# Moving the third gate and up group of a slot ahead of k and q, from tile 8 on, in a fused retention and feed-forward block

## What is computed

```python
q1, k1 = x @ Wq, x @ Wk                 # 4 heads of 64, then rotary
v = x @ Wv                              # 4 heads of 128
o = chunk_retention(q * 64 ** -0.5, k, v, gamma)
o = rmsnorm(o, gn_weight) * silu(x @ Wg)
x = layernorm(x + o @ Wo)
h = silu(x @ wg.T) * (x @ wu.T)         # 768 hidden, int weights / 127
x = layernorm(x + h @ wd.T)
```

## Time and profile before

| | |
|---|---|
| median of 3 runs | 443.9 us (443.34 to 444.12) |
| the profiled execution's own time | 444.02 us |
| its span, first to last instruction | 442.2 us |
| PE busy | 428.2 us (97%) |
| PE weight loads busy | 400.4 us (91%) |
| DVE busy | 302.1 us (68%) |
| ACT busy | 295.7 us (67%) |
| POOL busy | 238.9 us (54%) |
| mean granted TensorE clock | 0.997 |

### The profile page before, as it was taken

One profiled execution on the slowest core, in us unless ns is written; L12 is line 12 of the kernel. 1 busy time (PEld: TensorE's weight loads), 2 busy tenths in 40 slices (PEclk: granted clock), 3 DMA queues, 4 the chain that ended last, 5 costly groups with the idle time before them and its releaser, 6 DMA issues.

```text
span 442.2 us, 10997 instructions
## 1 busy us (share of the span) xinstructions
PE 428.2 (97%) x3552; PEld 400.4 (91%) x3552; DVE 302.1 (68%) x857; ACT 295.7 (67%) x891; POOL 238.9 (54%) x381
## 2 busy tenths in 40 slices
PE   7989999999999999999999999999999999999994
PEld 3878889999999999999999999999999999999983
DVE  4989566657766776666776667677666667766774
ACT  5678766657766767765776676686676667665541
POOL 2654255755555465453766446564655546554564
PEclk9999999999999999999999999999999999999998
DMA  7931000011100111110111101011110000100011
GB/s 241 363 134 50 0 29 22 24 38 37 38 11 27 37 38 38 37 37 0 36 36 36 36 27 44 0 36 36 36 36 13 15 22 14 38 12 13 14 38 39
DMA packets 16228, 19.60 MB, mean 44 GB/s; under 512 B 1472, under 2 KB 13760, under 8 KB 16192
## 3 DMA queue, kind: packets, MB, share of 16 engines
q1 hardware_dynamic: 16192, 19.14, 13.2%
HBM read 14.94 MB, written 4.19 MB: 43 GB/s over the span
## 4 chain that ended last, share of the span: by engine, by line
PE 85%; DVE 8%; issue 3%; POOL 1%; ACT 1%; DMA 1%; SPq 0%; POOLq 0%; DVEq 0%; ACTq 0%
PE b_rows L440 28%; PE b_ffn L440 18%; PE b_rows L458 8%; PE b_rows L454 6%; PE b_head L587 6%; PE b_head L555 3%; PE b_state L440 3%; PE b_head L558 3%; PE b_turn L615 3%; PE b_ffn L576 2%; PE b_turn L468 2%; DVE y L1316 1%; DMA wf_int<-in_w_proj 1%; DVE qk L1172 1%; DVE rot_s L1159 1%
## 5 line engine op out<-in xcount | busy, mean ns | idle before, releaser
L1509 POOL TENSOR_TENSOR h_lo<-wf_int,h_hi 128x256 fp32r<-128x256 f32 x96 | 71.0, 740 | 76.5 <-ACT h_hi L951 76.2
L440 PE MATMUL b_ffn<-x1T_hi,wf_hi 128*128 128x256 f32 x384 | 93.2, 279 | 1.0 <-DVE x1T_lo L1295 1.0
L440 PE MATMUL b_ffn<-x1T_lo,wf_hi 128*128 128x256 f32 x384 | 92.5, 278 | 0.0
L440 PEld LDWEIGHTS b_ffn<-x1T_hi,wf_hi 128*128 128x128 f32 x384 | 72.2, 188 | 2.1 <-DVE x1T_lo L1295 1.6
L440 PEld LDWEIGHTS b_ffn<-x1T_lo,wf_hi 128*128 128x128 f32 x384 | 72.3, 188 | 0.3
L915 ACT ACTIVATE sq<-b_head 128x128 f32<-128x128 f32 x124 | 34.4, 277 | 54.7 <-PE b_head L587 51.7
L1534 POOL TENSOR_TENSOR ve<-mv,eps 128x1 f32<-128x1 f32 x64 | 14.2, 222 | 93.7 <-DVE mv L1337 87.3
L940 ACT ACTIVATE wf_int<-b_ffn 128x256 f32<-128x256 f32 x96 | 36.8, 383 | 32.8 <-PE b_ffn L440 32.6
L951 ACT CAST h_hi<-wf_int 128x256 fp32r<-128x256 f32 x96 | 38.8, 405 | 19.1 <-DVE wf_int L1249 18.2
L1328 DVE TENSOR_TENSOR z<-b_rows,x_sb 128x256 f32<-128x256 f32 x32 | 13.5, 423 | 55.4 <-PE b_rows L440 55.4
L1249 DVE TENSOR_TENSOR wf_int<-b_ffn,wf_int 128x256 f32<-128x256 f32 x96 | 40.1, 418 | 15.5 <-ACT wf_int L940 11.2
(11 more groups left out here) (154 smaller groups left out, 1320.2 us busy)
## 6 DMA issues: line engine op xcount, KB each, us to landing
xT_raw<-in_xT SPq DMA_DIRECT2D x16, 256.0 KB, 3.1
x_sb<-in_x SPq DMA_DIRECT2D x16, 256.0 KB, 2.7
out<-wf_int SPq DMA_DIRECT2D x32, 128.0 KB, 1.7
wf_int<-in_w_ffn SPq DMA_DIRECT2D x6, 384.0 KB, 7.6
wf_int<-in_w_proj SPq DMA_DIRECT2D x6, 256.0 KB, 5.2
rope_sb<-in_rope SPq DMA_DIRECT2D x4, 256.0 KB, 6.6
rope_q<-in_rope_by_row SPq DMA_DIRECT2D x2, 512.0 KB, 9.4
wo_raw<-in_w_o SPq DMA_DIRECT2D x1, 512.0 KB, 6.8
```

Source lines behind the costliest of these rows:

```text
L440: mm = pe.matmul(dst, a, b, start=(i == 0 and j == 0 and not begun), stop=(i == n - 1 and j == len(passes) - 1 and not more), skip_group_c ...
L1509: pool.tensor_tensor(h_lo[:, ring, hb], h_full[:, u], h_hi[:, ring, hb].bitcast(F32), ALU.subtract).then_inc(h_split[j], 1)
```

## The change

Only the order changes, in three of the engines' lists, and only in slots 8 to 31. On PE the third gate and up group comes in front of k and q. On ACT its SiLU comes in front of the rounding of the x tile three slots ahead. On DVE its hidden product comes in front of the rotations.

```diff
                 down(s - 1, q1, t1, wide)
                 if natural(s):
                     project(s, q, t, 1, v_done)
-                else:
-                    keys_and_queries(s, q, t)
                 if is_slot(s, 0):
                     warm(FILL)
                 gate_up_block(s - 1, q1, t1, 2, wide)
+                if not natural(s):
+                    keys_and_queries(s, q, t)
                 recall_and_score(s, q, t)
                 turn_x1(s, q, t)
                 turn_y(s, q, t)
...
                 keep_x1(s, q, t)
                 if is_slot(s, NATURAL):
                     split_xT(s + 2, *back(q, t, -2))
+                gate(s - 1, t - 1, 2)
                 if exists(s + 3):
                     split_xT(s + 3, *back(q, t, -3))
-                gate(s - 1, t - 1, 2)
                 if is_slot(s, NATURAL):
                     copy_first_q()
                 turn_q(s, q, t, 0)
...
                 hidden(s - 1, t - 1, 1)
                 residual_2(*prev)
                 stats_2(*prev)
+                hidden(s - 1, t - 1, 2)
                 rotate_k(s, q, t)
                 rotate_q(s, q, t)
                 moments_2(s - DOWN_LAG - 1, back(q, t, DOWN_LAG + 1)[1], waited=has_q(s, t))
-                hidden(s - 1, t - 1, 2)
                 mask(s, q, t)
```

## The result

The changed kernel takes 445.65 us (median of 9 runs, 444.94 to 446.30) against 443.87 us before (9 runs, 443.21 to 444.40). The ratio estimated from all runs is 1.0045, with a 95% interval of 1.0036 to 1.0054; the medians lie 1.8 us apart, the kernel after being the slower. The forecast was 445.9, from 443.8 to 447.3.

What follows compares the result with a forecast made beforehand. PE was taken as the bound, busy 428.2 of 442.2 us. From the profiled 444.02 us, 1.9 of stalls in five slots plus 0.7 in slot 9, less 0.7 of pace, gave 445.9 us; 8-in-10 range 443.8 to 447.3.

Steps and rivals of the forecast that it cites:

- The bound: Steady slots on PE: no wait ends last there, so reordering gains only through matmul pace and loses through late results.
- The pace: Third gate and up group on PE, no longer behind the q block: 0.04 us gained per slot, 0.7 over 17 slots.
- the first rival: Faster: handover of x1T_lo not late, pace and step before recall both improve; -2.4 us, 441.6; chance 0.07.
- The stall in slots 13 to 25: First gate and up group's weight load waits for x1T_lo in t = 1 slots: 0.38 us each, 1.9 for five slots.
- lower bound by the q block alone: Slots 13 to 29 with t = 1: rotation 0.56 us late from the q block, a stall of 0.23 each.
- Slot 9: Already stalling, no reserve: the rotation starts 0.7 us later, all of it lost.
- the second rival: Nothing to measure: 5 x 0.23 + 0.56 = 1.7 us lost against 0.7 to 2.4 gained, middle 444.2; chance 0.18.
- Slot 29: Counted among the five t = 1 slots stalling at the first gate and up group, 0.38 us like the others.
- The plain slots: 17 slots with t other than 1: some 0.2 us of reserve at the first gate and up group, costed at nothing.
- The output projection: Waits for q's second turn and yT_lo, later in t = 1 slots; taken as covered, else 0.3 us more each.
- The waits list: Profile after: b_ffn weight load waits for x1T_lo six times or so, near 3 us, against 1.6 in two.
- The sum: Whole kernel: 444.02 + 1.9 + 0.7 - 0.7 = 445.9 us; this forecast had chance 0.68.

Runs made afterwards that it cites:

- q_before_k: Kernel before, with k projected behind q on PE; 444.6 us, a single run.
- q_as_k: Kernel before, with the q block's six matmuls replaced by six in k's form (tokens held, weights moved), q then wrong from tile 8; 445.1 us, a single run.
- pe_only: Kernel before, with the changed order on PE alone, ACT and DVE keeping their order; 444.66 us, ratio to before 1.0013.
- engines_only: Kernel after, with PE put back to the order of before, ACT and DVE staying changed; 459.4 us, a single run.
- x1T_first_t1: Kernel after, but in t = 1 slots ACT makes x1T_hi ahead of its first turn of q; 444.17 us, ratio to before 1.0006.
- t1_old: Kernel after, but t = 1 slots keep the old order on PE, ACT and DVE; 443.25 us, ratio 0.9977.
- silu_sooner: Kernel after, with ACT's copy to x1_late moved behind the SiLU of the third group; 444.84 us, ratio to before 1.0016.
- k_next_to_recall: Kernel after, with k projected behind q, so k stands next to recall; 445.6 us, a single run.

## Why the prediction was right

- **The bound.** "A reordering can gain only through the pace of the matmuls. It can lose by letting a result come too late": both happened, each where it was placed.
- **The pace.** 0.04 a slot was forecast and measured (13.31 to 13.27). It was put down to slot 31's missing q block, and `q_before_k` and `q_as_k` bear that out, though "the slow pace follows the q block" holds for everything behind it until recall, not for its neighbour alone. The 109 ns for 256 columns that the prediction took from the Trainium skill, "TensorE: Matmul & The Clock Gate", section "Back-to-back issue gap", come from a formula with the number of columns alone in it; that section calls it the gap of an isolated matmul and says that in a stream the weight loads help to set the spacing. These runs don't agree with it as a pace of a stream: 256 columns took 0.113 or 0.119 at the same granted clock (mean 0.995 to 0.999). The other half of the first rival, a shorter step before recall, didn't come: 0.21 stayed, in slot 17 before the scores (215.48 to 215.69), in plain slots before recall (0.20 to 0.21).
- **The stall in slots 13 to 25.** Forecast 0.38, measured 0.39 a slot. Rotation 0.71 late by forecast, 0.70 by the trace; release 0.06 after `x1T_lo`, by the trace 218.68 to 218.74. The lower bound by the q block alone, 0.23, is about what `pe_only` cost (0.26).
- **Slot 9.** Forecast 0.7, measured 0.70, and by the product, as forecast. But the second rival let the q block alone cost 0.56 there; `pe_only` shows that it costs nothing in slot 9, so that rival's 1.7 us of loss were too much (`pe_only` lost 1.3 in the five others). The forecast doesn't rest on it, the lower end of its range in part does.
- **Slot 29.** Forecast 0.38 as the others, measured 0.27: the term that was mis-sized, by 0.1 us. Slot 29 is not slot 17 on DVE, and the trace of before had it: there the stats start 5.13 us after the slot's start and `x1T_lo` 7.80, against 5.30 and 7.96 in slot 17, so that the reserve was 0.16 larger. After, the stats start at 5.14 (371.83 - 366.69), the product no longer comes last, and the rotation starts where the q block alone puts it in `pe_only`, at 6.20. Why DVE is earlier in this slot stays open.
- **The plain slots.** Forecast no stall with 0.2 in reserve. In slot 15 of the kernel after `x1T_lo` starts at 192.28 and ends at 192.70, and the weight load stands at 192.92, 0.22 later. With 0.06 for the release that leaves 0.16 of reserve, and no wait. `engines_only` shows what it costs when this cover is gone.

```profile
192.28 0.42 DVE L1295 TENSOR_TENSOR x1T_lo<-b_ffn,x1T_hi 128x256 fp32r<-128x256 f32 x1 [0.46 <-ACT x1T_hi L885]
```

```profile
192.92 0.19 PEld L440 LDWEIGHTS b_ffn<-x1T_hi,wf_hi 128*128 128x128 f32 x1
```

- **The output projection**, costed at nothing. It held: in slot 17 of the kernel after, the projection follows GU0 by the plain 0.11. Once GU0 no longer stalled (`x1T_first_t1`), the second turn and `yT_lo` were late for it, by 0.19.
- **The waits list.** Forecast near 3 us in six times or so, measured 3.9 in seven: the list grew by 2.3 us from 1.6, somewhat less than the 2.5 by which the six slots grew.
- **The sum.** 1.9 + 0.7 - 0.7 = 1.9 forecast; 1.86 in the trace from slot 9 to slot 31, 1.81 with slot 8, whose gain the forecast counts too; 1.78 between the medians. The closeness is not the cancelling of large errors: no term was off by more than 0.1 us (the five stalls 1.9 forecast and 1.82 measured, with slot 29 in them; the gain 0.7 forecast and 0.71 measured, with slot 8).

## What to carry to other kernels

On an engine that is never idle, ask of each reordering which results are now just in time, and do it for the shortest iteration, not for a typical one: here all of the loss was in the six of 24 slots that have less PE work to hide behind. Follow the late result through each in-order queue: the handover that stalled PE had no part in the change, its first half (`x1T_hi`) only stood on ACT behind a turn of q that had become late. A reorder that pays in most iterations and costs in a few can be made in the former alone (`t1_old`).

## What the runs showed of the hardware that was not expected

- PE has two paces for matmuls of 256 columns at the same granted clock, 0.113 and 0.118 to 0.119 us, and can stay at the slow one across blocks of another kind. It was seen behind the q block until recall, or until the scores where t = 1, wherever a block of 256 columns stood there; and in the output projection, in some slots and not in others, behind a stall: 1.41 to 1.42 us for its twelve matmuls in slots 13 and 17 of `silu_sooner`, slot 9 of `t1_old` and slot 25 of `k_next_to_recall`, 1.36 to 1.37 in most others. In `x1T_first_t1` it began in the output projection of slot 17 (1.49 us) and lasted through the 512-column matmuls of the next v projection, GU1, `down`, GU2, k and q, until the recall of slot 18. What starts it stays open.
- The first step behind a stall is long: in slot 17 of the kernel after, the first two matmuls of GU0 start 0.22 apart (218.75 and 218.97), and in `x1T_first_t1` the first two of the output projection 0.19. That, not the slow pace, makes up most of the 1.45 to 1.46 us that this block took in slots 13, 21, 25 and 29 of the latter.
- Single times can mislead by more than the effect sought. In the run of `q_as_k`, 445.1 us, slots 10 to 30 were shorter than before, but slot 9 began at 106.37 instead of 104.32: what comes ahead of slot 8, where the two kernels do the same, took 2 us more. Where a few tenths of a microsecond a slot are at stake, the length of a slot in the timeline is the better measure.

```profile
106.37 0.48 PE L454 MATMUL b_rows<-wp_hi,xT_hi 128*128 128x512 f32 x1
```
